# Two-layer graph attention on one core: gathering the neighbours of row blocks 0 to 2 in two portions, split by source column

## Chip, cores and metric

One core of a Trainium2 chip runs the whole kernel. The metric is device time in microseconds (us). PE is TensorE, DVE VectorE, ACT ScalarE, POOL GpSimd and SP SyncE, which here only starts transfers.

## The reference, cut to what matters

```python
N, D, H = 2048, 512, 16
x = layernorm(x + gnn0(x, adj, pairs, Wq, bq, Wk, bk))   # first layer: neighbour mean, corrected for few listed pairs
seq = (x @ W_seq).reshape(N, H, 32)
s1, s2 = einsum('nhd,d->hn', seq, a1), einsum('nhd,d->hn', seq, a2)
scores = leaky_relu(s1[:, :, None] + s2[:, None, :], 0.2) + (1 - adj) * -65500
hidden = einsum('hij,jhd->ihd', softmax(scores), seq).reshape(N, 512) @ W_out + b_out
out = layernorm(x + elu(hidden))
```

`adj` is 2048 x 2048 with ones on the diagonal and else about 4 ones in a row of 2048. In the second layer row i needs the rows of `seq` (and the score s2) of its neighbours j only.

## The kernel before, in words

The 2048 rows are 16 row blocks of 128 (one row per partition). Engines work from written-out queues and meet at semaphores. The stages, in order of time:

- **Listing and first product (0 to about 153 us).** SP loads the rows of `adj`. ACT casts a block to f16 (`cast_row`, L1006), PE transposes it (`turn_rows`, L621), ACT copies the transposed block out of PSUM (`save_turned`, L1015), and PE multiplies it with x (`multiply`, L639). Beside it DVE lists each row's neighbours (`listing`: `list_keys`, `list_rest`, `list_top`): the f16 key of column j is j+1, MAX8 finds the largest 8 of each eighth of the row, and `list_top` finds the largest 8, strikes them out (MATCH_REPLACE8) and finds the next 8. They go to `ek`. The f16 row buffer has two halves, so ACT casts block b only when block b-2 is listed (`row_listed`) and turned. POOL fetches adjacency values for the 10,000 pairs, 79 gathers of one value per partition (L530), and every group of 6 of them waits for a count of finished products (`ax_made`). `count_pairs` on DVE waits for the last of them, and most of what follows until the flag that says whether the sparse path can be used (`flag_made`) hangs on it.
- **Norm stage (about 157 to 231 us).** For each of the 16 blocks PE transposes the normed rows, computes `seq` with the scores s1 and s2 in 16 matmuls (`make_seq`, L841) and spreads the list of the block before over the partitions (`spread_keys`, L851). ACT saves the result, and SP stores each block of `seq` with s2, 528 f32 per row, to the table `seqtab` in device memory (L475). DVE norms rows, makes the span masks for the spreading (`make_key_span`) and, for four blocks at a time, the gather indices `eidx` (`pick_edges`). A block's 128 rows have at most KE x 128 = 512 neighbours beyond the first of each row. They are packed into four tiles of 128, one neighbour per partition; the first (nearest) neighbour of each row has a tile of its own, whose partition is the row itself (`near`). So a block takes GE = 5 gathers of 128 rows.
- **Second layer (from about 231 us).** POOL waits until all 16 blocks are in `seqtab` and then issues 5 indirect gathers for each block in turn (L607), into one of GR = 3 buffers. Block b from 3 on waits also until PE has summed block b-3 (`e_agg`). For a block DVE computes the arguments of the exponential (`arguments`, L1970, L1973, L1978), ACT takes the exponential (L1229, L1231), DVE multiplies the gathered rows by the weights (`weigh`, L2006, in lots), lays the row's own share and adds the nearest tile in PSUM (`own_share` L1929, `add_nearest` L1936), PE sums the packed tiles through one-hot matrices (L955, made by `one_hots` L1845), and DVE divides (`finish`, L1940 and L1942). `W_out`, ELU and the last norm follow some blocks behind (`add_elu`, L1876, L1878). Block 0 is done in two parts, its first three tiles ahead of the last two. At the start, `self_args` and `largest` (L1947 to L1964) make the largest scores.

## Time and profile before

| | us |
|---|---|
| time, median of 3 (lowest to highest) | 394.93 (393.57 to 396.96) |
| time of the profiled execution | 395.34 |
| its span | 393.5 |
| PE, DVE, ACT, POOL busy | 344.1, 322.2, 199.8, 186.6 |
| mean granted TensorE clock (1 is full speed) | 0.968 |

The profile is of one execution, the one of 395.34 us. Its span goes from the first to the last recorded instruction; 1.84 us lie around it. Times within it are counted from its start. A row of the timeline gives start, duration, engine, line, operation, what is written and read, how many instructions are merged, and in square brackets how long the engine had been idle before and what released it.

### The profile page before, as it was taken

The numbers are of one execution on the slowest core, as the hardware profiler recorded it, in microseconds if no ns is written. First come the engines' busy times: TensorE is split into PE (matmuls) and PEld (weight loads), VectorE is DVE, ScalarE is ACT, GpSimd is POOL, SyncE is SP. The second block draws the span as 40 slices with busy tenths as digits, with TensorE's granted clock in tenths as the row PEclk, the third lists the DMA queues.
The fourth block names the chain that finished last, engine by engine and source line by source line (L and its number), as shares of the span: only waits on it lengthen the run. The fifth ranks groups of instructions, "written<-read, shape, count | busy, mean of one in ns | idle before, by whom it ended". The sixth has DMA issues, their size and how long they took to land.

```text
span 393.5 us, 5227 instructions
## 1 busy us (share of the span) xinstructions
PE 344.1 (87%) x1656; PEld 213.8 (54%) x1656; DVE 322.2 (82%) x816; ACT 199.8 (51%) x449; POOL 186.6 (47%) x178
## 2 busy tenths in 40 slices
PE   0899899999999988999999934699989999999970
PEld 0444645555444644788888813456545655665540
DVE  2999999985978477777988687778899999999772
ACT  3975874466430224555654321122446776677780
POOL 7776558777771000000000047888778878770000
PEclk9999999999999999999999975899999999999995
DMA  6999464436994402921111237665675776662014
GB/s 250 373 384 378 177 214 121 185 126 160 229 231 92 145 0 66 383 106 66 57 55 57 82 110 209 177 171 161 172 191 164 201 215 209 182 205 82 27 56 142
DMA packets 34758, 65.10 MB, mean 165 GB/s; under 512 B 15649, under 2 KB 16801, under 8 KB 32673
## 3 DMA queue, kind: packets, MB, share of 16 engines
q1 hardware_dynamic: 25632, 42.45, 32.1%
q0 software_dynamic: 9088, 22.20, 20.5%
q8 instruction: 17, 0.28, 0.3%
q14 instruction: 21, 0.16, 0.1%
HBM read 53.50 MB, written 8.52 MB: 158 GB/s over the span
## 4 chain that ended last, share of the span: by engine, by line
PE 41%; DVE 26%; POOL 13%; issue 7%; ACT 6%; DMA 5%; SPq 0%; DVEq 0%; ACTq 0%; POOLq 0%
PE ps L639 17%; PE ps L841 15%; POOL adjT L607 9%; DVE adjT L2006 8%; POOL pr L530 5%; DMA arenaA<-in_x_dram 2%; DVE arenaC L1878 2%; DVE adjT L1876 2%; DVE ps L1936 2%; DVE arenaA L1942 2%; DVE ps L1929 2%; PE ps L621 2%; PE ps L830 2%; DVE arenaB L1845 2%; ACT adjT L1015 1%
## 5 line engine op out<-in xcount | busy, mean ns | idle before, releaser
L639 PE MATMUL ps<-arenaB,adjT 128*128 128x512 f16 x512 | 115.6, 379 | 2.7 <-ACT adjT L1015 1.6
L530 POOL DMA_INDIRECT pr<-in_adj_dram,aidx x79 | 82.0, 1038 | 30.6 <-issue 23.0
L607 POOL DMA_INDIRECT adjT<-seqtab,eidx x64 | 77.2, 1206 | 19.5 <-issue 19.5
L955 PE MATMUL ps<-adjT,arenaB 128*128 128x264 f32 x256 | 67.9, 412 | 18.5 <-DVE adjT L2006 14.1
L639 PEld LDWEIGHTS ps<-arenaB,adjT 128*128 128x128 f16 x512 | 48.8, 98 | 59.9 <-ACT adjT L1015 3.2
L607 POOL DMA_INDIRECT adjT<-seqtab,near x16 | 21.5, 1341 | 107.6 <-DMA seqtab<-arenaA 102.9
L955 PEld LDWEIGHTS ps<-adjT,arenaB 128*128 128x128 f32 x256 | 49.4, 200 | 41.1 <-DVE ps L1936 21.1
L841 PE MATMUL ps<-stage 128*128 128x272 f32 x256 | 61.5, 394 | 0.1
L868 PE MATMUL ps<-adjT 128*128 128x512 f32 x120 | 54.1, 593 | 1.0 <-ACT ps L1135 1.0
L841 PEld LDWEIGHTS ps<-stage 128*128 128x128 f32 x256 | 47.4, 190 | 9.5 <-ACT stage L1104 0.8
L2006 DVE TENSOR_TENSOR adjT<-adjT 128x1024 f32<-128x1024 f32 (+2 forms) x35 | 47.9, 1373 | 2.3 <-ACT adjT L1231 1.9
L1006 ACT ACTIVATE halves<-stage 128x2048 f16<-128x2048 f32 x16 | 30.8, 1922 | 13.2 <-DMA stage<-in_adj_dram 6.1
L868 PEld LDWEIGHTS ps<-adjT 128*128 128x128 f32 x120 | 21.6, 190 | 22.8 <-issue 21.5
L1015 ACT COPY adjT<-ps 128x1024 f16<-128x1024 f16 x20 | 19.2, 1014 | 21.5 <-PE ps L621 21.5
L1323 DVE TENSOR_TENSOR arenaA<-iota,halves 128x2048 f16<-128x2048 f16 x15 | 18.3, 1223 | 7.5 <-ACT halves L1006 7.4
L1135 ACT COPY ps<-adjT 128x512 f32<-128x512 f32 x15 | 8.8, 590 | 30.4 <-DVE adjT L1876 30.4
L621 PE MATMUL ps<-identh,halves 128*128 128x128 f16 x176 | 13.2, 235 | 9.7 <-ACT halves L1006 9.7
L1330 DVE MAX8 arenaA<-arenaA 128x8 f16<-128x256 f16 x60 | 21.1, 414 | 0.5
L1229 ACT ACTIVATE stage<-stage 128x80 f32<-128x80 f32 (+2 forms) x17 | 4.4, 258 | 32.9 <-DVE stage L1978 32.9
L1335 DVE MAX8 arenaA<-arenaA 128x8 f16<-128x256 f16 x60 | 20.8, 411 | 0.0
L1110 ACT COPY arenaA<-ps 128x256 f32<-128x256 f32 x32 | 11.9, 375 | 14.8 <-PE ps L841 14.8
L621 PEld LDWEIGHTS ps<-identh,halves 128*128 128x128 f16 x176 | 12.1, 106 | 12.1 <-issue 9.1
(277 smaller groups left out, 486.7 us busy)
## 6 DMA issues: line engine op xcount, KB each, us to landing
stage<-in_adj_dram SPq DMA_DIRECT2D x16, 1024.0 KB, 6.1
seqtab<-arenaA SPq DMA_DIRECT2D x16, 264.0 KB, 2.0
arenaA<-in_x_dram SPq DMA_DIRECT2D x4, 1024.0 KB, 12.0
out_dram<-arenaC SPq DMA_DIRECT2D x16, 256.0 KB, 3.5
arenaB<-in_x_dram SPq DMA_DIRECT2D x1, 1536.0 KB, 10.6
pr<-in_adj_dram,aidx POOLq DMA_INDIRECT x79
arenaC<-in_L_gnn_Wq_dram SPq DMA_DIRECT2D x1, 1024.0 KB, 16.6
arenaC<-in_L_gnn_Wk_dram SPq DMA_DIRECT2D x1, 1024.0 KB, 20.0
```

The lines of the kernel that those rows point to most:

```text
L530: g.indirect_dma_start(out=avals[:, t:t + 1], out_offset=None, in_=adj_flat, in_offset=bass.IndirectOffsetOnAxis(ap=aidx[:, t:t + 1], axis ...
L607: g.indirect_dma_start(out=Grow[:, b % GR, k, :], out_offset=None, in_=seqtab, in_offset=bass.IndirectOffsetOnAxis(ap=source, axis=0)).the ...
L621: ins = t.transpose(turn_banks(b)[:, j, :], arowh[:, b % 2, j * P:(j + 1) * P], identh[:])
L639: ins = t.matmul(bank(4 + b % 2), adjT[:, b, j, :], xsplit[:, w, j, :], start=(j == 0 and w == 0), stop=(j == NB - 1 and w == 1))
L841: ins = t.matmul(half_bank(n), xT[:, b % 2, k, :], Wx[:, k, s, :], start=(k == 0), stop=(k == KT - 1))
L868: ins = t.matmul(bank(6 + b % 2), hT[:, b % 2, k, :], Wo[:, k, :], start=False, stop=(k == KT - 1), skip_group_check=True)
L955: ins = t.matmul(bank(2 * (b % 2) + c, HALF), ehot[:, b % HOTS, k - 1, :], Grow[:, b % GR, k, c * HALF:(c + 1) * HALF], start=False, stop= ...
L1006: s.activation(arowh[:, b % 2, :], arow[:, b % 2, :], ACT.Identity, accum_out=deg[:, 0, b:b + 1]).then_inc(row_cast, 1)
L1015: s.copy(adjT[:, b, 8 * k:8 * k + 8, :], turn_banks(b)[:, 8 * k:8 * k + 8, :]).then_inc(row_evac, 1)
L1330: v.max(top[:, 0, 8 * k:8 * k + 8], key[:, k * SEG:(k + 1) * SEG])
L1335: ins = v.max(top[:, 0, 8 * k:8 * k + 8], key[:, k * SEG:(k + 1) * SEG])
L2006: v.tensor_tensor(some[:, :, 0:D1], some[:, :, 0:D1], some[:, :, D1:HW].to_broadcast([P, (last - first) * H1, D1]), ALU.mult).then_inc(e_m ...
```

## The change

The neighbours of row blocks 0, 1 and 2 (`EARLY` = 3) are split by column. Those in the first `CUT` = 13 blocks of columns ("low") fill the nearest tile and the first three packed tiles, those in the last three blocks ("high") the fourth packed tile.

- POOL waits for the first 13 stores of the table (a semaphore of their own, `tab_first`) and issues the 4 low gathers of each of the three blocks. Then it waits for the last three stores and issues one high gather for each. Blocks 3 to 15 are gathered as before.
- For blocks 0 to 2, `list_top` has two more instructions, which turn the key j+1 into 2048-j, so that the lowest columns rank first. A new function `split_lists` (13 instructions) counts the low neighbours of each row, and turns the keys back.
- The counts that PE sums (`count_rows`) have three more columns, `measure` and `judge` one and two more instructions, `make_key_span` one for blocks 0 to 2, `pick_edges` one for the first group. The spread list has a column more (51 for 50).
- In the second layer blocks 0 to 2 are done in two parts, the four low tiles and the high one. The start is in another order: the arguments of block 0 come ahead of what the row's own share needs, and DVE waits for the whole table only after them. The one-hots of blocks 3 to 5 move from ahead of block 0 into blocks 0 to 2, and one call of `largest` from block 2 to block 3.

```diff
             def list_top(b, top=top, junk=junk):
...
-                link(v.max(ek[:, b, 0:8], top[:, 0]))
-                link(v.match_replace(top[:, 1], ek[:, b, 0:8], top[:, 0], 0.0))
-                v.max(ek[:, b, 8:16], top[:, 1])
+                found, rest = top[:, 0], top[:, 1]
+                if b < EARLY:
+                    link(v.tensor_scalar(top[:, 1], top[:, 0], -1.0, N + 1.0, ALU.mult, ALU.add))
+                    link(v.scalar_tensor_tensor(top[:, 1], top[:, 0], 0.0, top[:, 1], ALU.is_gt, ALU.mult))
+                    found, rest = top[:, 1], top[:, 0]
+                link(v.max(ek[:, b, 0:8], found))
+                link(v.match_replace(rest, ek[:, b, 0:8], found, 0.0))
+                v.max(ek[:, b, 8:16], rest)
...
             listing(NB - 2)
+            split_lists()
             list_keys(NB - 1)
...
                 def make_key_span(b):
...
+                    n = KE * P
+                    if b < EARLY:
+                        n -= P
+                        v.tensor_scalar(span[:, b % 2, n:], iota[:, n:n + P], hend[:, 0, b:b + 1], hend[:, 1, b:b + 1],
+                                        ALU.max, ALU.min)
...
-                pool.wait_ge(tab_store, 16 * NB)
-                for b in range(NB):
+                pool.wait_ge(edges_made, 1)
+                pool.wait_ge(tab_first, 16 * CUT)
+                for b in range(EARLY):
+                    for k in range(KE):
+                        gather(b, k, e_low[b])
+                pool.wait_ge(tab_store, 16 * (NB - CUT))
+                for b in range(EARLY):
+                    gather(b, KE, e_high[b])
+                for b in range(EARLY, NB):
                     if b % 4 == 0:
                         pool.wait_ge(edges_made, b // 4 + 1)
-                    if b >= GR:
-                        pool.wait_ge(e_agg, b - GR + 1)
+                    pool.wait_ge(e_agg, b - GR + 1)
                     for k in range(GE):
...
-                    for b in range(3, 6):
-                        one_hots(b)
-                    own_share(0)
-                    for lo, hi in parts_of(0):
-                        dve.wait_ge(e_first[lo // FEW], 16 * (hi - lo))
-                        arguments(0, lo, hi)
-                        weigh(0, lo, hi)
-                    for b in range(1, NB):
-                        if b == 1:
+                    for b in range(EARLY):
+                        dve.wait_ge(e_low[b], 16 * KE)
+                        arguments(b, 0, KE)
+                        if b == 0:
+                            self_rest()
+                            table_stored(dve)
+                            late(v.memset(seq[:, :, :, D1:HW], 1.0))
+                            self_parts()
+                            own_share(0)
+                        one_hots(EARLY + b)
+                        if b == 2:
+                            own_share(2)
+                        weigh(b, 0, KE)
+                        dve.wait_ge(e_high[b], 16)
+                        arguments(b, KE, GE)
+                        if b == 0:
                             own_share(1)
-                        dve.wait_ge(e_gather[b % GR], 16 * GE * (b // GR + (b % GR > 0)))
+                        else:
+                            finish(b - 1)
+                        weigh(b, KE, GE)
+                    for b in range(EARLY, NB):
+                        dve.wait_ge(e_gather[b % GR], 16 * GE * (b // GR))
                         arguments(b, 0, GE)
```

The queues show this at three places. On DVE, the end of a block's listing in the first stage, here block 1; `arenaA` holds the 64 candidate keys, `ekb` the list. Before:

```order
L1340 TENSOR_REDUCE over<-arenaA 128x1
L1341 MAX ekb<-arenaA 128x8
L1342 MATCH_REPLACE arenaA<-ekb,arenaA 128x64
L1343 MAX ekb<-arenaA 128x8
L1344 ISA arenaA,deg<-halves,identh 128x128
L1344 ISA deg 128x1
```

After, at the same place:

```order
L1365 TENSOR_REDUCE over<-arenaA 128x1
L1368 TENSOR_SCALAR arenaA<-arenaA 128x64
L1369 SCALAR_TENSOR_TENSOR arenaA<-arenaA 128x64
L1371 MAX ekb<-arenaA 128x8
L1372 MATCH_REPLACE arenaA<-ekb,arenaA 128x64
L1373 MAX ekb<-arenaA 128x8
L1374 ISA arenaA,deg<-halves,identh 128x128
L1374 ISA deg 128x1
```

Two instructions of 64 elements stand between the reduction and the first MAX, for blocks 0, 1 and 2 each.

On POOL, the first gathers of the second layer; `near` is the nearest tile, `eidx` a packed one. Before:

```order
L607 DMA adjT<-seqtab,near 128x528 [waits edges_made,tab_store]
L607 DMA adjT<-seqtab,eidx 128x528 x4
L607 DMA adjT<-seqtab,near 128x528
L607 DMA adjT<-seqtab,eidx 128x528 x4
L607 DMA adjT<-seqtab,near 128x528
L607 DMA adjT<-seqtab,eidx 128x528 x4
L607 DMA adjT<-seqtab,near 128x528 [waits e_agg]
```

After:

```order
L615 DMA adjT<-seqtab,near 128x528 [waits tab_first,edges_made]
L615 DMA adjT<-seqtab,eidx 128x528 x3
L615 DMA adjT<-seqtab,near 128x528
L615 DMA adjT<-seqtab,eidx 128x528 x3
L615 DMA adjT<-seqtab,near 128x528
L615 DMA adjT<-seqtab,eidx 128x528 x3
L615 DMA adjT<-seqtab,eidx 128x528 [waits tab_store]
L615 DMA adjT<-seqtab,eidx 128x528 x2
L615 DMA adjT<-seqtab,near 128x528 [waits e_agg]
```

Twelve of the fifteen gathers now wait for 13 stores, and three for all 16; the first gather of block 3 still waits for block 0's sums.

On DVE, the start of the second layer, from the first wait for gathered rows to the first weighing of block 1. Before (block 0 in parts of 3 and 2 tiles):

```order
L1970 TENSOR_TENSOR stage<-arenaB,adjT 128x48 [waits e_first0]
L1973 SCALAR_TENSOR_TENSOR stage<-stage 128x48 [waits sp_arg]
L1978 TENSOR_TENSOR stage<-stage,arenaB 128x48 [waits mxe_made,sp_arg]
L2006 TENSOR_TENSOR adjT<-adjT 128x16x32 [waits e_exp]
L1936 TENSOR_TENSOR ps<-ps,adjT 128x2x264 [waits e_mul,own_laid]
L2006 TENSOR_TENSOR adjT<-adjT 128x16x32 x2
L1970 TENSOR_TENSOR stage<-arenaB,adjT 128x32 [waits e_first1]
```

After (the part of 4 tiles, with what now stands inside it):

```order
L2043 TENSOR_TENSOR stage<-arenaB,adjT 128x64 [waits e_low0]
L2046 SCALAR_TENSOR_TENSOR stage<-stage 128x64 [waits sp_arg]
L2051 TENSOR_TENSOR stage<-stage,arenaB 128x64 [waits mxe_made,sp_arg]
L2020 TENSOR_TENSOR arenaB<-arenaB 128x256
L2022 TENSOR_SCALAR arenaB<-arenaB 128x256 [waits self_arg]
L2086 MEMSET arenaA 128x256 [waits tab_store,tab_first]
L2027 TENSOR_TENSOR arenaB<-arenaB,deg 128x256 [waits self_exp,late_link]
L1993 TENSOR_TENSOR ps<-arenaA,arenaB 128x2x264 [waits opened,self_kept]
L1909 TENSOR_TENSOR arenaB<-iota,erow 128x512
L2074 TENSOR_TENSOR adjT<-adjT 128x16x32 [waits e_exp]
L2000 TENSOR_TENSOR ps<-ps,adjT 128x2x264 [waits e_mul,own_laid]
L2074 TENSOR_TENSOR adjT<-adjT 128x16x32 x3
```

The own-share preparation moves behind the arguments of block 0, and one one-hot build (L1909) stands there for three.

## Rows read from the trace of the kernel before

**Rows 1.** Stretches: core us, busy us (instructions) by engine, clock, DMA share, GB/s.

```profile
231.40:278.10 46.70, 32.34 (x115) 22.33 (x116) 36.37 (x66) 8.19 (x21) 36.98 (x32) 0.82 0.63 178
...
290.00:360.00 70.00, 66.95 (x242) 41.66 (x241) 67.83 (x108) 47.21 (x128) 51.32 (x40) 1.00 0.64 186
```

**Rows 2.** Timeline of DVE: first of the second layer, arguments of blocks 3, 4, 5.

```profile
231.44 0.42 DVE L1947 TENSOR_TENSOR arenaB<-scores,M 128x256 f32<-128x256 f32 x1 [0.76 <-DVE M L1906]
...
262.11 0.30 DVE L1970 TENSOR_TENSOR stage<-arenaB,adjT 128x80 f32<-128x80 f32 x1 [2.14 <-DMA adjT<-seqtab,eidx]
...
269.23 0.30 DVE L1970 TENSOR_TENSOR stage<-arenaB,adjT 128x80 f32<-128x80 f32 x1 [0.95 <-DMA adjT<-seqtab,eidx]
...
278.09 0.30 DVE L1970 TENSOR_TENSOR stage<-arenaB,adjT 128x80 f32<-128x80 f32 x1 [1.36 <-DMA adjT<-seqtab,eidx]
```

**Rows 3.** Timeline of POOL: first gather of blocks 0, 3, 4, 5, 6.

```profile
230.45 0.97 POOL L607 DMA_INDIRECT adjT<-seqtab,near  x1 [102.87 <-DMA seqtab<-arenaA]
...
250.22 2.18 POOL L607 DMA_INDIRECT adjT<-seqtab,near  x1 [0.30 <-issue]
...
259.41 0.95 POOL L607 DMA_INDIRECT adjT<-seqtab,near  x1 [0.30 <-issue]
...
266.03 2.17 POOL L607 DMA_INDIRECT adjT<-seqtab,near  x1 [0.31 <-issue]
...
275.63 0.95 POOL L607 DMA_INDIRECT adjT<-seqtab,near  x1 [0.30 <-issue]
```

**Rows 4.** DMA issues (count, KB each, us to landing); SP's timeline, last four stores.

```profile
seqtab<-arenaA SPq DMA_DIRECT2D x16, 264.0 KB, 2.0
adjT<-seqtab,eidx POOLq DMA_INDIRECT x64, 3.9
...
215.65 12.84 SPq L475 DMA_DIRECT2D seqtab<-arenaA  x4
```

**Rows 5.** Timeline, a gather beside a weighing; POOL's group of the first stage (busy us, mean ns).

```profile
247.87 1.23 DVE L2006 TENSOR_TENSOR adjT<-adjT 128x1024 f32<-128x1024 f32 x1 [0.71 <-ACT adjT L1231]
248.33 1.59 POOL L607 DMA_INDIRECT adjT<-seqtab,eidx  x1 [0.30 <-issue]
...
L530 POOL DMA_INDIRECT pr<-in_adj_dram,aidx x79 | 82.0, 1038 | 30.6 <-issue 23.0
```

**Rows 6.** Last stretch of the norm stage, columns as in Rows 1.

```profile
216.00:228.00 12.00, 11.72 (x64) 9.40 (x62) 8.31 (x30) 4.22 (x18) 0.00 (x0) 1.00 0.18 68
```

**Rows 7.** DVE groups by shape, 231.4 to 278.1 us: count, busy us, mean ns.

```profile
L1929 DVE TENSOR_TENSOR ps<-arenaA,arenaB 128x528 f32<-128x528 f32 x5 | 3.6, 717 | 0.0
...
L2006 DVE TENSOR_TENSOR adjT<-adjT 128x512 f32<-128x512 f32 x5 | 3.3, 697 | 1.2 <-ACT adjT L1231 1.2
```

**Rows 8.** Timeline of PE: block 0's 16 matmuls of packed tiles.

```profile
241.08 5.91 PE L955 MATMUL ps<-adjT,arenaB 128*128 128x264 f32 x16 [10.05 <-DVE adjT L2006]
```

**Rows 9.** Timelines of DVE, ACT, PE and POOL, 31 to 52 us, engine by engine.

```profile
35.56 0.22 DVE L1341 MAX8 ekb<-arenaA 128x8 f16<-128x64 f16 x1
35.81 0.09 DVE L1342 MATCH_VALUE_LOAD arenaA<-ekb,arenaA 128x8 f16 x1
...
36.48 0.08 DVE L1344 DVE_READ_ACCUMULATOR2_ANT deg<- 128x1 f32 x1
...
31.41 1.91 ACT L1006 ACTIVATE halves<-stage 128x2048 f16<-128x2048 f32 x1 [0.72 <-DVE deg L1344]
...
36.67 1.91 ACT L1006 ACTIVATE halves<-stage 128x2048 f16<-128x2048 f32 x1 [3.26 <-PE ps L621]
...
40.55 1.04 PE L639 MATMUL ps<-arenaB,adjT 128*128 128x512 f16 x4 [1.37 <-ACT adjT L1015]
...
51.91 0.95 POOL L530 DMA_INDIRECT pr<-in_adj_dram,aidx  x1 [5.53 <-PE ps L639]
```

**Rows 10.** Timeline of DVE around the listing of the last block.

```profile
116.43 1.23 DVE L1323 TENSOR_TENSOR arenaA<-iota,halves 128x2048 f16<-128x2048 f16 x1 [2.14 <-ACT halves L1006]
...
119.89 0.24 DVE L1365 TENSOR_TENSOR arenaA<-prf 128x79 f32<-128x79 f32 x1 [0.54 <-DMA pr<-in_adj_dram,aidx]
```

More of the change, by code:

```diff
@@ L47, in two_layer_graph_attention @@
     GR = 3
-    KW = 18 + 32
-    FEW = 3
+    KW = 18 + 32 + 1
+    EARLY = 3
+    CUT = NB - 3
     HOTS = 8
@@ L300, in parts_of, with nth_part, table_stored @@
         def parts_of(b):
-            return ((0, FEW), (FEW, GE)) if b == 0 else ((0, GE),)
+            return ((0, KE), (KE, GE)) if b < EARLY else ((0, GE),)
+        def nth_part(b, lo):
+            return sum(len(parts_of(a)) for a in range(b)) + 1 + (lo > 0)
+        def table_stored(eng):
+            eng.wait_ge(tab_first, 16 * CUT)
+            eng.wait_ge(tab_store, 16 * (NB - CUT))
         def lots_of(b):
-            return tuple((k, k + 1) for k in range(GE)) if b == 0 else ((0, 2), (2, GE))
+            if b == 0:
+                return tuple((k, k + 1) for k in range(GE))
+            return ((0, 2), (2, KE), (KE, GE)) if b < EARLY else ((0, 2), (2, GE))
         def weighed(b, k):
@@ L714, in count_rows @@
                 pe.wait_ge(cnt_made, 1)
-                t.matmul(ps[:, 3, 0:NB], below[:], mv[:, :, 0], start=True, stop=True)
-                t.matmul(ps[:, 3, NB:2 * NB], ones[:], mv[:, :, 0], start=True, stop=True)
+                n = NB + EARLY
+                t.matmul(ps[:, 3, 0:n], below[:], counts[:, 0, :], start=True, stop=True)
+                t.matmul(ps[:, 3, n:2 * n], ones[:], counts[:, 1, :], start=True, stop=True)
                 pe.wait_ge(u_saved, 1)
@@ L1231, in act_second_layer @@
                             s.activation(G[:, b % GR, lo * H1:hi * H1, D1], a2, ACT.Exp, scale=-1.0).then_inc(e_exp, 1)
+                            if n == 1:
+                                act.wait_ge(self_made, 1)
+                                s.activation(sa[:, 2], sa[:, 1], ACT.Exp).then_inc(self_exp, 1)
                         if b >= 2:
@@ L1830, in pick_edges @@
                         link(ins)
+                        if c == 0:
+                            last = spot[:, 0].rearrange("p (q k) -> p q k", q=4)[:, 0:EARLY, KE - 1]
+                            starts = sp_.rearrange("p (q k) c -> p q k c", q=4)[:, 0:EARLY, KE - 1, KW - 1]
+                            link(v.scalar_tensor_tensor(last, rowid[:, KE - 1:KE].to_broadcast([P, EARLY]), 2.0, starts,
+                                                        ALU.add, ALU.subtract))
                         link(v.tensor_tensor(pick[:, 0], kiota.unsqueeze(1).to_broadcast([P, 4 * KE, 16]),
```

96 lines of the change are left out of this document (60 added, 36 removed).

## The prediction

> **What bounds the kernel now.** I read the stretches first, then the waits of DVE and POOL, then the chain of waits back from the end. The second layer is the part that the change speaks of. In its first 46.7 us, to 278.1, DVE is busy for 36.4 us and POOL is issuing nearly all the time; from 290 to 360 us DVE is busy for 67.8 of 70 us [rows 1]. So this layer has two bounds, one behind the other. At first it is the issue of gathers: DVE reaches the arguments of blocks 3, 4 and 5 and waits 2.14, 0.95 and 1.36 us for the last gather [rows 2], while POOL, which waited for the last store until 230.45, sits only 0.30 us between two gathers [rows 3]. From block 6 on no argument waits for a gather, and DVE's own work sets the pace. Whatever makes block 5's arguments start earlier than 278.09 is therefore passed on to the end, and what comes earlier only on POOL is not.
>
> Ahead of the second layer the norm stage is PE's: 11.72 of 12 us busy, while DVE has 8.31 and POOL nothing [rows 6]. In the first stage one chain matters for the edits there, and I come to it below.
>
> **The gathers, part by part.** SP issues the last four stores from 215.65, so block 12's is the one at 215.65; a store lands in 2.0 us [rows 4]. The low gathers can start at 215.65 + 2.0 + 0.3 = 217.95 instead of 230.45, 12.5 us earlier. A gather and the gap behind it take 0.95 + 0.30 = 1.25 us when nothing disturbs it [rows 3], so the 12 low ones would end at 233.0. One that starts while DVE multiplies two operands out of SBUF is held: at 248.33 a gather began inside a weighing that ended at 249.10, and took 1.59 us, to 0.82 after that end [rows 5]. The norm stage has such instructions too, but short ones. I take 0.1 us a gather, as in the first stage, where 79 gathers took 1.04 us in the mean beside DVE's listing [rows 5], hence 234.2; by bounds 0 and, if each met one of 0.72 us [rows 7], 0.7 us a gather, 241.4. The three high gathers follow, and 3.9 us after its issue [rows 4] the first has landed, at 238.1. DVE asks for it at about 241.5 (below): not late.
>
> DVE's side now. From 231.44 block 0 costs: five instructions of 0.42 (L1947 and its like) 2.1; arguments 0.8; the four that prepare the own share, up to 0.42 each, and ACT's exponential between them 2.0; own share 0.7, one one-hot build, taken as an own share, 0.7; the nearest tile 0.7 and its addition 0.7; the first packed tile 0.7. That is 239.8, and PE can begin its sums. Then two more tiles at 0.7, the arguments of the high tile 0.6 (at 241.8), the next own share 0.7 and the high tile 0.7: block 0 leaves DVE at 243.2 [rows 2, 7]. Block 1 is two sets of arguments 1.4, one-hots 0.7, weighing 1.2 + 1.2 + 0.7, the addition 0.7 and a division 0.9, together 6.8; block 2 the same with an own share, 7.5. So DVE alone would be at block 3's arguments at 257.5. Block 3 took 269.23 - 262.11 - 0.95 = 6.2 us without its wait, and gets the moved call of `largest`, 0.8; block 4 took 278.09 - 269.23 - 1.36 = 7.5 [rows 2]. DVE alone would begin block 5 at 257.5 + 7.0 + 7.5 = 272.0, 6.1 us earlier than before.
>
> But POOL is in it again, through the three buffers: block 3 is gathered only when PE has summed block 0. PE's 16 matmuls for it took 5.91 us [rows 8], in a stretch whose mean granted clock is 0.82 [rows 1]. From 239.8 they end at 245.7, and POOL begins block 3 at 246, 4.2 us earlier than 250.22 and not 12.5. Before, the first six blocks took (275.63 - 230.45)/6 = 7.5 us each on POOL, and blocks 3 to 5 8.5, since a denser DVE holds more gathers [rows 3]; I take 7.8. Block 5's first gather is at 246 + 15.6 = 261.6. From its first gather to its arguments a block needed 11.9, 9.8 and 12.1 us (blocks 3, 4, 5) [rows 2, 3], mean 11.3: 272.9. That is later than DVE's own 272.0, so POOL decides, by a little, and the gain is 278.09 - 272.9 = 5.2 us. The best that it can be is 6.1, DVE's own; with 8.5 us a block and 12.1 behind it 275.1, a gain of 3.0; with block 0's sums no earlier than before (247) and POOL's worst block, 266.03 to 275.63, three times over, 278.3, none.
>
> **What it costs ahead of that.** The two instructions in `list_top` are linked, each waiting for the one before. The step from one linked instruction on 64 elements to the next is 0.25 us, from 35.56 to 35.81 [rows 9]; two of them, 0.45 (the first overlaps the reduction), in three blocks 1.35 us by 36.5 us. This DVE time is on the path. ACT may cast block 4 only when block 2 is listed: DVE's last instruction of that listing ends at 36.56 and the cast starts at 36.67. The row gives PE as the releaser, because a transpose ends in the same moment, but the cast needed only transposes long done; the cast of block 3, at 31.41, names DVE [rows 9]. Behind the cast stand ACT's copy of block 3's transpose, and PE, which waits 1.37 us for it until 40.55; behind PE's block 3 the pair gathers, which stood for 5.53 us until 51.91. From there POOL issues them at its own pace to the last, and DVE waits for that one's landing until 119.89 [rows 9, 10]. None of these has slack, so I let 1.35 us through to the end; by bounds 0, if some of it finds a gap that I do not see, and 1.7, a quarter more.
>
> `split_lists` is 13 instructions. Its cover is in two waits: DVE stood for 2.14 us before the last listing and for 0.54 us before `count_pairs`, 2.68 in all [rows 10]. The instructions are on 3 to 48 elements, eight of them linked; at 0.2 and 0.1 they make 2.2 us, at 0.25 each 3.3. So 0 to 0.6 comes out; I take 0.1. The additions to `measure` and `judge` stand behind the flag's inputs and beside PE's last product: 0, by bounds up to 0.3. The extra span instruction for blocks 0 to 2 sits at the start of the norm stage, where DVE is only just ahead of PE: 0.15 us, by bounds 0 to 0.5. The extra instruction in `pick_edges` and the wider lists find DVE with a third of its time free and cost nothing; without that cover they would be 0.2.
>
> The sum is 395.34 - 5.2 + 1.35 + 0.1 + 0.15 = 391.7 us for the profiled execution. That execution was 0.4 above the median of the runs, so a median would be 391.3 by the same steps. I say 391.4, 0.9% below 394.93.
>
> **A rule weighed.** Beside gathers DVE's own instructions were no longer than without: own share, addition and one-hots run at 0.7 us with POOL issuing. The Trainium skill, page "SBUF — State Buffer", section "Who interferes with whom", states that VectorE and GpSimd share a port pair under an exclusive lock, that whoever issues first has it for the whole instruction, and that a `tensor_tensor` contends only with what GpSimd reads. The held gather agrees as far as POOL is the loser [rows 5]; for DVE as the loser no row shows a case, and by that half of the rule the moved gathers would lengthen the norm stage. It is the last rival.
>
> **Rivals.** First, the listing is hidden: the wait view is right that the cast of block 4 was PE's, or PE's later waits take the 1.35 us up. For it speaks the releaser in the row, against it the missing slack behind. Then 395.34 - 5.2 + 0.25 = 390.4, by the median 390.0.
>
> Second, the issue of gathers keeps the bound: the held gathers of blocks 3 to 5 stay as in the rows, 8.5 us a block, or block 0's sums come no earlier because PE is as slow and starts later. The gain is 3.0 or less, on average 1.7: 395.3. From 1.6 us of gain down the change is no gain at all. For it speaks that POOL is never idle before and that a denser DVE holds it more; against, that it then has the pause from 238 to 246.
>
> Third, and slower: the high gather of block 0 is late. It stands behind 12 low ones, and DVE has block 0's high tile, the next own share and all of block 1 queued behind that wait. If every low gather meets a DVE instruction of 0.7 us, the first high one is issued at 241.4, and with a landing drawn out to 5 us beside the last stores and held itself for 1.2 us it is there at 248, 6 us after 241.8. That takes the whole gain, and 1.6 us of cost stays: 397. It decides from about 3.6 us of lateness on, a landing at 245.4.
>
> Fourth, DVE is the loser of the lock: each of 12 gathers holds up one DVE instruction by up to 0.95 us, 11.4 us, of which the 12 us stretch hides 12 - 8.3 = 3.7 [rows 6]. The norm stage then ends 7.7 us later: 399. With half of that blocking, 2.0 us later, the time would be 393.7.
>
> **How the numbers follow.** Forecast 0.50, listing hidden 0.14, issue-bound 0.24, late high tile 0.06, DVE held 0.06. The forecast's own range is 390.0 to 393.0. A measurement of this kernel tells about 1% from no change, 3.9 us, and 1% faster is 391.0, close under the forecast: I give the forecast 0.24 of its 0.50 there, the hidden listing all of its 0.14, and the issue-bound case none, which makes 0.38 for faster by over 1%. Slower by over 1% (above 398.9) needs most of the fourth rival or more than the third's price: 0.04. The rest, 0.58, is within 1%. The range of 8 in 10 goes from 389.4, a little under the hidden listing, to 395.6, which takes in the issue-bound case.
>
> **What would show it.** POOL's first gather of the table some 12 to 13 us before the last block's store lands, and 12 gathers of about 1.3 us with their gaps. Then a pause of POOL of 6 to 9 us, ended by PE's sums of block 0. DVE's arguments of blocks 1 and 2 without a wait for a gather, and those of block 5 some 40.5 to 42.5 us behind the layer's first instruction, where it was 46.65. The cast of block 4 at 38.0 for 36.67, and `count_pairs` at 121.2 for 119.9. The start of the second layer at about 233.0 for 231.44. The forecast is wrong if that start is not later (listing hidden), if it is over 3 us later (DVE held), or if block 5's arguments still come 45 us or more behind it.

## The result, and the profile after

| | before | changed |
|---|---|---|
| time, median (lowest to highest), us | 395.28 (393.57 to 396.96), 4 runs | 2285.93 (2284.49 to 2286.89), 4 runs |
| time and span of the profiled execution | 395.34, 393.5 | 2284.49, 2282.7 |
| mean granted TensorE clock | 0.968 | 0.570 |

The ratio is 5.781 (95% interval 5.762 to 5.800). Times here and below are medians of all runs, while a ratio takes only those runs of each kernel that lie within 1.5% of its fastest, so it can differ from the ratio of the medians. The prediction was 391.4 us, 389.4 to 395.6, with 0.04 on slower. No case of it comes near.

This is the changed kernel's page: its span, the first section's busy times, the clock of section 2 in 40 slices, four groups of section 5, and one row of the DMA issues.

```profile
span 2282.7 us, 23174 instructions
PE 2054.1 (90%) x9616; PEld 1921.5 (84%) x9616; DVE 1780.3 (78%) x1558; ACT 162.0 (7%) x305; POOL 88.2 (4%) x98
...
PEclk9999555555555555555555555555555555555587
...
L920 PE MATMUL ps<-arenaB 128*128 128x33 f32 x8192 | 1751.0, 402 | 146.4 <-DVE arenaB L2164 146.4
...
L2164 DVE TENSOR_TENSOR arenaB<-arenaB,adjT 128x2048 f32<-128x2048 f32 x256 | 586.7, 2292 | 131.2 <-PE ps L920 122.1
L2159 DVE SCALAR_TENSOR_TENSOR arenaB<-stage,arenaB 128x2048 f32<-128x2048 f32 x256 | 601.8, 2351 | 9.1
L2157 DVE TENSOR_SCALAR arenaB<-stage,arenaB 128x2048 f32<-128x2048 f32 x256 | 329.4, 1287 | 17.0 <-DMA stage<-etab 6.5
...
stage<-etab SPq DMA_DIRECT2D x32, 1024.0 KB, 5.5
```

Read it for what is there and for what is not. PE has 8192 records from one line that the kernel before never reached, in 256 batches of 32 (16 heads by 16 source blocks); `etab` is a table that only the dense second layer writes. No row of any view has `seqtab` as the source of a gather, so nothing of what [rows 3] show happens at all, early or late. The kernel took the other branch of its second layer: the flag that says "the lists do not fit, work with the whole matrix" was up. That dense branch stands in the kernel before too, and had not run there.

Up to the branch the trace is the predicted one, a little late. Below are the changed kernel's casts of blocks 3 and 4 and the restart of the pair gathers, which answer to [rows 9], the first use of the gathered pairs [rows 10], the copy that closes the norm stage, and the first instruction of the dense layer.

```profile
32.79 1.91 ACT L1030 ACTIVATE halves<-stage 128x2048 f16<-128x2048 f32 x1 [0.46 <-DVE deg L1374]
...
38.56 1.91 ACT L1030 ACTIVATE halves<-stage 128x2048 f16<-128x2048 f32 x1 [3.76 <-DVE deg L1374]
...
53.80 0.94 POOL L545 DMA_INDIRECT pr<-in_adj_dram,aidx  x1 [5.64 <-PE ps L662]
...
122.40 0.24 DVE L1414 TENSOR_TENSOR arenaA<-prf 128x79 f32<-128x79 f32 x1 [0.40 <-DMA pr<-in_adj_dram,aidx]
...
233.12 0.17 DVE L1970 COPY M<-ps 128x16 f32<-128x16 f32 x1
237.07 0.43 DVE L2134 TENSOR_TENSOR arenaB<-scores,M 128x256 f32<-128x256 f32 x1 [3.78 <-issue]
```

The same copy in the kernel before:

```profile
230.51 0.17 DVE L1906 COPY M<-ps 128x16 f32<-128x16 f32 x1
```

So 2.6 of the 1890 us are front cost, and all the rest lies behind the copy, from which the changed kernel needs 2049.6 us to its end, and the kernel before 163.0. From 400 us to the end, says the stretch below, PE is busy for 1707 of 1882 us at a mean clock of 0.52.

```profile
400.00:2282.00 1882.00, 1707.17 (x7811) 1661.62 (x7811) 1470.67 (x878) 38.82 (x68) 0.00 (x0) 0.52 0.05 19
```

**Why the flag is up.** `judge` raises it when a row block has more than KE * P = 512 listed neighbours beyond the nearest. The count comes from `count_rows`, which multiplies `counts` with a matrix of ones, and so adds it up over the 128 partitions. `split_lists` adds a constant to `counts` on every partition, to fold the two portions' own limits into the one test: 128.0 for the low portion, 384.0 for the high. Summed over 128 partitions these are 16384 and 49152. Both are above 512 whatever the graph is. What was meant is 128 and 384 on the sum of a block. An excess of 128 over the block is 1.0 a partition, one of 384 is 3.0, KE - 1. With these the test reads low + 128 > 512 and high + 384 > 512, which is what three tiles and one tile hold. The input fits: blocks 0 to 2 have 295, 259 and 312 low extra neighbours (room for 384) and 81, 104 and 88 high ones (room for 128), and the largest block has 428.

### The profile page after: what moved, and what is told of

It reads as the page before. It is cut to its first block, busy times and chain, and to the rows that moved or that the text cites. A ratio compares the mean times of both kernels' runs of the same rounds, so it can differ in the third digit from the quotient of the medians.

```text
span 2282.7 us, 23174 instructions
## 1 busy us (share of the span) xinstructions
PE 2054.1 (90%) x9616; PEld 1921.5 (84%) x9616; DVE 1780.3 (78%) x1558; ACT 162.0 (7%) x305; POOL 88.2 (4%) x98
## 4 chain that ended last, share of the span: by engine, by line
PE 85%; DVE 7%; issue 2%; ACT 2%; POOL 1%; DMA 1%; DVEq 0%; SPq 0%; ACTq 0%; POOLq 0%
PE ps L920 77%; PE ps L892 3%; PE ps L865 2%; DVE arenaB L2159 2%; DVE arenaB L2164 2%; POOL pr L545 1%; PE ps L662 1%; DVE arenaB L2157 1%; DMA arenaA<-in_x_dram 0%; ACT adjT L1168 0%; ACT ps L1159 0%; ACT adjT L1150 0%; DVE arenaA L2173 0%; DVE arenaB L1343 0%; PE ps L912 0%
## 5 line engine op out<-in xcount | busy, mean ns | idle before, releaser
L920 PE MATMUL ps<-arenaB 128*128 128x33 f32 x8192 | 1751.0, 402 | 146.4 <-DVE arenaB L2164 146.4
L920 PEld LDWEIGHTS ps<-arenaB 128*128 128x128 f32 x8192 | 1748.8, 333 | 148.9 <-DVE arenaB L2164 148.9
L2164 DVE TENSOR_TENSOR arenaB<-arenaB,adjT 128x2048 f32<-128x2048 f32 x256 | 586.7, 2292 | 131.2 <-PE ps L920 122.1
L2159 DVE SCALAR_TENSOR_TENSOR arenaB<-stage,arenaB 128x2048 f32<-128x2048 f32 x256 | 601.8, 2351 | 9.1
L2157 DVE TENSOR_SCALAR arenaB<-stage,arenaB 128x2048 f32<-128x2048 f32 x256 | 329.4, 1287 | 17.0 <-DMA stage<-etab 6.5
L892 PE MATMUL ps<-adjT 128*128 128x512 f32 x128 | 70.9, 706 | 35.9 <-ACT adjT L1150 35.9
L892 PEld LDWEIGHTS ps<-adjT 128*128 128x128 f32 x128 | 27.3, 223 | 70.2 <-issue 37.1
L1940 DVE SCALAR_TENSOR_TENSOR adjT<-ps,adjT 128x512 f32<-128x512 f32 x16 | 11.1, 691 | 81.2 <-ACT adjT L1170 81.2
L1854 DVE BATCH_NORM_STATS2 stats<-arenaC 128x6 f32<-128x512 f32 x32 | 22.2, 694 | 1.1
L1355 DVE MAX8 arenaA<-arenaA 128x8 f16<-128x256 f16 x60 | 21.1, 414 | 0.5
## 6 DMA issues: line engine op xcount, KB each, us to landing
arenaB<-in_x_dram SPq DMA_DIRECT2D x1, 1536.0 KB, 10.7
```

The costliest lines, as they stand in the source:

```text
L892: ins = t.matmul(bank(6 + b % 2), hT[:, b % 2, k, :], Wo[:, k, :], start=False, stop=(k == KT - 1), skip_group_check=True)
L920: ins = t.matmul(ps[:, b // 8, (b % 8) * (D1 + 1):(b % 8 + 1) * (D1 + 1)], p_buf[:, j % 2, b * P:(b + 1) * P], seqh[:, j, :], start=(j == ...
L1355: v.max(top[:, 0, 8 * k:8 * k + 8], key[:, k * SEG:(k + 1) * SEG])
L1854: link(v.bn_stats(stats[:, b, :], x1[:, b, :]))
L2157: v.tensor_scalar(p_raw, eB[:, 0, :], Fh[:, 0, j:j + 1], None, ALU.mult).then_inc(L.sem, 1)
L2159: v.scalar_tensor_tensor(p_raw, eB[:, 1, :], Fh[:, 1, j:j + 1], p_raw, ALU.mult, ALU.max).then_inc(L.sem, 1)
```

## The experiments

**e1, both constants mended.**

```diff
-                v.tensor_scalar_add(counts[:, 1, 0:EARLY], counts[:, 0, 0:EARLY], float(P))
+                v.tensor_scalar_add(counts[:, 1, 0:EARLY], counts[:, 0, 0:EARLY], 1.0)
...
-                v.tensor_scalar_add(counts[:, 1, NB:NB + EARLY], counts[:, 0, NB:NB + EARLY], float((KE - 1) * P))
+                v.tensor_scalar_add(counts[:, 1, NB:NB + EARLY], counts[:, 0, NB:NB + EARLY], float(KE - 1))
...
+                        gather(b, k, e_low[b], CUT * P)
```

(The last line names only the first 13 blocks of the table as the source of the low gathers; the rows they fetch are the same. It is part of e1 and of e5 to e12. It can't have to do with the flag, since no gather of the table runs while the flag is up.)

> The changed kernel with the added numbers 128 and 384 in split_lists replaced by 1 and 3 (both are added on each of 128 partitions and then summed over the partitions), and the low gathers given the first 13 blocks of the table as their source. Theory A (the sum over partitions makes 128 x 128 out of the 128, so the count is always over the limit of 512, and the kernel takes its dense path): the sparse path is back, about 391 to 393 us, with POOL's first table gather near 220 us. Theory B (the split lists do not fit their tiles for these data, or the sparse path of the change is itself slow): 2286 us again, or far over 400 us. Rival within A: the gain of the early gathers is eaten by the front (count_pairs was 2.5 us later in the changed kernel): 395 us.

Measured: 391.24 us (390.01 to 392.93), ratio 0.9895 (0.9866 to 0.9925). 1895 us are gone with two numbers, and the change as it was meant is 1.05% faster than the kernel before. The timeline of POOL and then of DVE, as in [rows 3] and [rows 2]:

```profile
222.03 0.95 POOL L615 DMA_INDIRECT adjT<-seqtab,near  x1 [91.78 <-DMA seqtab<-arenaA]
...
249.39 1.15 POOL L615 DMA_INDIRECT adjT<-seqtab,near  x1 [8.36 <-PE ps L979]
...
233.36 0.17 DVE L1970 COPY M<-ps 128x16 f32<-128x16 f32 x1
234.38 0.42 DVE L2011 TENSOR_TENSOR arenaB<-scores,M 128x256 f32<-128x256 f32 x1 [0.85 <-DVE M L1970]
...
258.91 0.30 DVE L2043 TENSOR_TENSOR stage<-arenaB,adjT 128x80 f32<-128x80 f32 x1 [0.17 <-DMA adjT<-seqtab,eidx]
...
266.06 0.31 DVE L2043 TENSOR_TENSOR stage<-arenaB,adjT 128x80 f32<-128x80 f32 x1 [0.20 <-DMA adjT<-seqtab,eidx]
...
275.08 0.30 DVE L2043 TENSOR_TENSOR stage<-arenaB,adjT 128x80 f32<-128x80 f32 x1 [1.52 <-DMA adjT<-seqtab,eidx]
```

The first gather is 12.35 us ahead of the layer's first instruction, POOL then stands for 8.36 us until PE has summed block 0, and block 5's arguments come 40.70 us behind the layer's start, where it was 46.65.

**e2, the low constant alone mended; e3, the kernel before with the limit set to 0** (nothing else of the change; its flag is up too).

```diff
-                link(v.tensor_scalar(bad[:, 2:3], bad[:, 2:3], float(KE * P), None, ALU.is_gt))
+                link(v.tensor_scalar(bad[:, 2:3], bad[:, 2:3], 0.0, None, ALU.is_gt))
```

> The changed kernel with only the first number mended (1 for 128), the 384 of the high counts left. Theory A: 384 x 128 = 49152 is over 512 by itself, so the dense path is still taken: 2286 us. Theory A', that only the low count raised the flag: about 392 us.

> The kernel before with the limit of the packed count at 0 for 512, so that its flag is always raised; nothing else is changed. Theory A: the whole of 2286 us is the dense path of the second layer, so this takes the changed kernel's time less what the change costs ahead of the second layer: 2283 to 2285 us. Theory B (something of the change is slow): clearly under 2280 us.

Measured: 2282.74 and 2284.10 us, one run each. The costliest group of e2's page, then that of e3's, whose line numbers are those of the kernel before:

```profile
L920 PE MATMUL ps<-arenaB 128*128 128x33 f32 x8192 | 1751.0, 402 | 146.5 <-DVE arenaB L2164 146.5
```

```profile
L896 PE MATMUL ps<-arenaB 128*128 128x33 f32 x8192 | 1751.0, 402 | 146.0 <-DVE arenaB L2086 146.0
```

So the 384 alone is enough to raise the flag. That the 128 alone would be follows from the same sum, 16384 over 512, and was not run. The whole excess is the dense branch's ordinary price, which the kernel before pays as well when it is sent there. The cause is settled. What follows asks whether the steps of the prediction hold for the change as it was meant.

**e4, the kernel before with the two linked instructions in the first three lists, and nothing else.**

```diff
+                if b < 3:
+                    link(v.tensor_scalar(top[:, 1], top[:, 0], -1.0, N + 1.0, ALU.mult, ALU.add))
+                    link(v.scalar_tensor_tensor(top[:, 1], top[:, 0], 0.0, top[:, 1], ALU.is_gt, ALU.mult))
```

> The kernel before with only the two linked 64-element instructions of list_top added for blocks 0 to 2, writing what nobody reads. If the listing is on the path as I predicted: 1.35 us more, 396.6 beside 395.3. If it is hidden: no change. If more is behind it (the changed kernel's count_pairs came 2.5 us later): 2.5 us more, 397.8.

Measured: 397.06 us against 395.35, ratio 1.0046 (1.0026 to 1.0066), +1.7 us. Cast, restart of the pair gathers, first use of the pairs, as in [rows 9, 10]:

```profile
38.05 1.91 ACT L1006 ACTIVATE halves<-stage 128x2048 f16<-128x2048 f32 x1 [3.76 <-DVE deg L1347]
...
53.29 0.94 POOL L530 DMA_INDIRECT pr<-in_adj_dram,aidx  x1 [5.63 <-PE ps L639]
...
121.33 0.24 DVE L1368 TENSOR_TENSOR arenaA<-prf 128x79 f32<-128x79 f32 x1 [0.50 <-DMA pr<-in_adj_dram,aidx]
```

All three are 1.38 to 1.44 us later than before, and so is the copy that closes the norm stage (231.90, 1.39 later). Nothing on the way takes any of it up. And the cast now names DVE as its releaser, where the row of before named a transpose that ended in the same moment.

This trace shows one thing more. Behind the copy e4 is the kernel before, instruction for instruction. Yet from the copy to the end of the span it needs 161.90 us and the kernel before 162.99, because other gathers met a weighing: those of blocks 3 to 5 took 5.1 us over 0.95 each in e4, and 6.6 us in the kernel before. Differences of about 1 us between two such stretches say nothing by themselves.

**e5 to e8, measured in one set.** That set ran under other conditions: the kernel before took 414.72 us in it (407.09 to 417.09, 17 runs), 5% more than in the other sets, and the first use of the gathered pairs, at 119.9 to 122.6 us in them, comes at 137.0 to 141.3 in the four profiles here. So their totals say little, and I read them from the copy that closes the norm stage to the end of the span. That stretch is 162.99 us in the kernel before (161.90 in e4) and 157.24 in e1. For the kernel before it is known only from the other set. The stretch carries over from one set to the other: e6 needs 155.91 us for it in this one, and its repetition e10, below, 156.10.

e5 lets the first gather wait for the whole table:

```diff
-                pool.wait_ge(tab_first, 16 * CUT)
+                table_stored(pool)
```

> The kernel of e1 with one line changed: the first gather of blocks 0 to 2 waits for all 16 stores of the table, not for the first 13. Everything else of the split (two portions of arguments and weights, the key and count edits) stays. Theory A, the gain is the early start alone: the first table gather moves from 222.03 to about 233.5 us, the 15 gathers of blocks 0 to 2 end 12 us later, block 5's arguments come 46 to 47 us behind the layer's first instruction as before, and the kernel costs before plus the front's cost: 396.5 to 398 us. Rival B, the gain comes from the new order of the DVE's work (own shares, self term, one-hots moved): it stays at 391 to 393 us.

Measured: 420.24 us, ratio 1.0221 (1.0100 to 1.0342); the stretch 166.69 us, 9.4 more than e1, with block 5's arguments 50.20 us behind the layer's start. DVE's waits for block 0's low and high portions:

```profile
259.89 0.27 DVE L2043 TENSOR_TENSOR stage<-arenaB,adjT 128x64 f32<-128x64 f32 x1 [5.32 <-DMA adjT<-seqtab,eidx]
...
271.11 0.19 DVE L2043 TENSOR_TENSOR stage<-arenaB,adjT 128x16 f32<-128x16 f32 x1 [4.23 <-DMA adjT<-seqtab,eidx]
```

e1 has neither. Rival B falls. The expectation of theory A was low too: without the early start the new order is not the old one back but 3.7 us worse (4.8 against e4's stretch), because block 0's high tile now stands behind twelve low ones. That is the third rival of the prediction, seen where the early start doesn't cover it.

e6 lists blocks 0 to 2 against numbers that run downwards, so that the two linked instructions go:

```diff
+            g.iota(iotar, [[-1, N]], base=N, channel_multiplier=0,
+                   allow_small_or_imprecise_dtypes=True).then_inc(rev_made, 1)
...
-                link(v.tensor_tensor(key, iota[:], arowh[:, b % 2, :], ALU.mult))
+                link(v.tensor_tensor(key, iotar if b < EARLY else iota[:], arowh[:, b % 2, :], ALU.mult))
```

> The kernel of e1, but the rows of blocks 0 to 2 are listed against a second table of numbers that runs downwards (made once by POOL in the first microseconds), so the two 64-element instructions in each of the three lists go. Theory A, these six instructions lie on the chain that starts POOL's 79 pair gathers: the casts come back to 31.4 and 36.7 us, the pair gathers start at about 51.9 instead of 53.2, and the time is 1.2 to 1.8 us below e1's 391.2, so 389.4 to 390.0. Rival B, the front has slack somewhere behind (for instance the landing of the last pair gather, which waited 2.04 us in e1): within 0.4 us of e1, 390.8 to 391.6.

Measured: 420.53 us, ratio 1.0267 (1.0180 to 1.0354). That says nothing on the listing, since e1 did not run in that set, and the kernel is repeated as e10. But its trace showed something new at the end of the norm stage (ACT, then DVE, which waits for it):

```profile
258.71 0.37 ACT L1138 COPY arenaA<-ps 128x256 f32<-128x256 f32 x1 [8.12 <-remote]
...
259.20 0.58 DVE L1963 TENSOR_REDUCE gm<-arenaA 128x16 f32<-128x256 f32 x1 [8.19 <-ACT arenaA L1140]
```

ACT stood for 8.12 us while the early gathers were out ("remote" is a releaser that this profile does not hold). e7 has the same stop with 7.37 us and e8 with 7.51; e5, without early gathers, has none, nor has e1. In this set none of the three kernels with the early start is faster than the kernel before (ratios 1.008 to 1.027), so the gain of e1 is shown for the other conditions only.

e7 takes blocks 1 and 2 in one portion. Beside changes of the order of DVE's work, the line that decides is:

```diff
-            return ((0, KE), (KE, GE)) if b < EARLY else ((0, GE),)
+            return ((0, KE), (KE, GE)) if b == 0 else ((0, GE),)
```

> The kernel of e1, but only block 0 is taken in two portions; blocks 1 and 2 wait for their high tile too and are worked in one piece, which saves DVE three 16-column instructions and one weighing instruction a block, about 0.55 us each, 1.1 together. In e1 the high tiles were there before block 1 began, so the wait costs nothing. Theory A, behind block 0 it is POOL, released by PE's sums of block 0, that sets the time: DVE reaches block 3's arguments 1.1 us earlier and waits 1.1 us more for its gathers, and the time stays within 0.4 us of e1: 390.8 to 391.6. Rival B, DVE sets the time: 390.0 to 390.4.

Measured: 417.89 us, ratio 1.0143 (0.9998 to 1.0289); the stretch 158.49 us. Block 3's arguments:

```profile
284.95 0.30 DVE L2043 TENSOR_TENSOR stage<-arenaB,adjT 128x80 f32<-128x80 f32 x1 [3.13 <-DMA adjT<-seqtab,eidx]
```

It spares DVE work and waits 3.13 us at the next gather, where e1 waited 0.17. DVE is ready for block 3 at 24.41 us behind the copy, 0.97 earlier than in e1, and gets it 1.99 us later, since block 3's five gathers were held for 2.40 us in all, for 0.37 in e1. Rival B falls: there is no gain. The stretch is 1.25 us longer, more than the 0.4 that theory A allowed, but not clear of the 1 us seen between equal stretches.

e8 keeps PE at work ahead of block 0's sums:

```diff
+                        if b == 0:
+                            pe.wait_ge(self_arg, 3)
+                            keep_warm(16)
                         pe.wait_ge(e_own, b + 1)
+                        if b == 0:
+                            keep_warm(8)
```

> The kernel of e1, with 24 matmuls of nobody's use (128x512, f16) on PE between the norm stage and block 0's sums, in a bank that is opened anew afterwards. In e1 PE stood idle there for 8.5 us and then worked off block 0's 16 matmuls at a granted clock of 0.50, 780 ns each where others take 386, ending at 249.1; POOL's block 3 waits for that. Theory A, this wait is the bound: with the clock at 1.00 block 0's sums end about 247, POOL's block 3 starts 2 us earlier, DVE's waits for gathers of blocks 3 to 5 (1.9 us in e1) all but go, and the time is 1.2 to 1.9 us below e1: 389.3 to 390.0. Rival B, DVE is the bound already and only waits elsewhere: 390.8 to 391.6.

Measured: 416.97 us, ratio 1.0077 (1.0004 to 1.0150); the stretch 157.79 us. The profile is of a run of 418.61 us, one of the longer of twelve. First block 0's sums in e1, with the stretch in which most of them ran (PE's busy time and count, granted clock, DMA share, GB/s), then the sums in e8, a gather of block 3 that was held, and DVE's arguments of block 5:

```profile
242.36 6.75 PE L979 MATMUL ps<-adjT,arenaB 128*128 128x264 f32 x16 [8.48 <-DVE adjT L2074]
...
244.00:248.00 4.00, 4.00 (x11) 0.50 0.00 0
```

```profile
269.18 3.72 PE L989 MATMUL ps<-adjT,arenaB 128*128 128x264 f32 x16
...
274.65 1.65 POOL L615 DMA_INDIRECT adjT<-seqtab,eidx  x1 [0.30 <-issue]
...
301.17 0.30 DVE L2053 TENSOR_TENSOR stage<-arenaB,adjT 128x80 f32<-128x80 f32 x1 [2.41 <-DMA adjT<-seqtab,eidx]
```

In e1 PE had stood for 8.48 us and worked most of them off at half of the full clock (1.2 of 2.4 GHz). In e8 the 16 matmuls take 3.72 us and not 6.75, and POOL's block 3 starts 14.06 us behind the copy and not 16.03: the first half of theory A is right. The gain is then lost. Of the lead of 1.97 us, 1.43 go in gathers of blocks 3 to 5 that are held for longer (5.69 us over 0.95 each in all, for 4.26), and the last gather of block 5 lands 3.80 us behind its end for 2.92. So block 5's arguments wait 2.41 us (1.52 in e1), and the stretch is no shorter. POOL issues without a pause from block 0's sums to block 5, but an earlier start is not passed on through that queue.

e9, the same kernel as e1 (below), says the same more closely. Its block 3 starts at 14.94 behind the copy, 0.88 later than e8's, and block 4 at 21.44 for 21.42: the whole difference is gone within five gathers.

**e9 to e12, measured in one set,** under the conditions of e1 again (before 395.05 us, 11 runs). e9 is e1's kernel and e10 is e6's. e11 issues only block 0's four low gathers early:

```diff
-                for b in range(EARLY):
-                    for k in range(KE):
-                        gather(b, k, e_low[b], CUT * P)
+                for k in range(KE):
+                    gather(0, k, e_low[0], CUT * P)
                 pool.wait_ge(tab_store, 16 * (NB - CUT))
-                for b in range(EARLY):
-                    gather(b, KE, e_high[b])
+                gather(0, KE, e_high[0])
+                for b in range(1, EARLY):
+                    for k in range(KE):
+                        gather(b, k, e_low[b])
+                    gather(b, KE, e_high[b])
```

and e12 is e10 with that edit.

> The kernel of e1, unchanged, beside the next three on one chip. The chip of e5 to e8 ran the kernel before in 414.7 us and not in 395.4, and three of its four profiles (those with early gathers) show ACT stopped for 7.4 to 8.1 us in the last block of the norm stage, while the twelve early gathers were out, with nothing in the profile that ends the stop; e1 showed none. Theory A, the stop is the early burst's work, on chips that are slow to serve it: on such a chip (before near 415) it is there again and e9 is 1 to 2% slower than before, on one like e1's (before near 395) it is absent and the ratio is 0.987 to 0.993 again. Rival B, the stop belongs to the edits of e6 to e8: e9 has none on any chip.

> The kernel of e6, now beside e9. Theory A, the six short listing instructions of blocks 0 to 2 lie on the chain that starts POOL's 79 pair gathers: 1.2 to 1.8 us below e9 on the same chip, 389.4 to 390.0 where before takes 395.4, with the casts at 31.4 and 36.7 us. Rival B, slack behind them: within 0.4 us of e9.

> The kernel of e1, but only block 0's four low gathers are issued inside the norm stage; the other eight and the three high ones wait for the whole table and go block by block. The burst shrinks from 15 us to 5, block 0's arguments still find their rows, and the 11 later gathers, issued from about the layer's start at 1.25 us each, should land before blocks 1 and 2 want them (11.7 and 18.3 us behind the copy of the maxima) and be out before block 0's sums end (16.0). Theory A, the early start pays through block 0 alone: the stretch from the copy of the maxima to the end stays within 1 us of e1's 157.2, and ACT's stop, where e9 shows one, is under 3 us. Rival B, the gain needs all twelve ahead: the stretch is 2 us or more longer and block 1 or 2 waits for gathers.

> e10 and e11 together. By theory A of both it has neither the listing's 1.4 us nor the long burst: 1.2 to 1.8 us below e11, and where before takes 395.4 it comes to 389.3 to 390.5; on a chip with the stop it is the first version that is not slower than before. By the rivals it is no faster than the better of e10 and e11.

| | time, us | ratio (95% interval) | copy to end, us |
|---|---|---|---|
| e9, mended | 391.03 | 0.9918 (0.9891 to 0.9944) | 156.78 |
| e10, reversed numbers | 389.58 | 0.9858 (0.9834 to 0.9882) | 156.10 |
| e11, four early | 391.51 | 0.9920 (0.9898 to 0.9942) | 157.40 |
| e12, both | 390.14 | 0.9878 (0.9852 to 0.9903) | 157.13 |

e9 repeats e1, and none of the four has ACT's stop. e10's cast of block 4 and its restart of POOL are back where [rows 9] have them:

```profile
36.66 1.91 ACT L1034 ACTIVATE halves<-stage 128x2048 f16<-128x2048 f32 x1 [3.26 <-PE ps L648]
...
51.90 0.95 POOL L549 DMA_INDIRECT pr<-in_adj_dram,aidx  x1 [4.38 <-PE ps L666]
```

and it is 1.45 us faster than e9: theory A, and the fastest kernel of this study, 1.4% under the kernel before. The difference is one of medians. In the profiled execution (390.86 us, the longest of five) the gain is lost again at the pairs, where the last gather took 1.95 us and first use is at 122.15. e12 against e11 shows the gain in the traces too: first use at 120.33 for 121.27, and the copy at 231.07 for 232.10. e11 shows how little of the early start is needed. POOL stops after four gathers and goes on with block 0's high one when the table is whole:

```profile
224.56 0.95 POOL L615 DMA_INDIRECT adjT<-seqtab,eidx  x1 [0.30 <-issue]
232.04 0.97 POOL L615 DMA_INDIRECT adjT<-seqtab,eidx  x1 [6.53 <-DMA seqtab<-arenaA]
```

No argument of blocks 0 to 4 waits for a gather, and the stretch is 0.6 us longer than e9's. e12 gains 1.37 over e11, but nothing over e10.

## Why the prediction was wrong, point by point

**The step that failed** is the one on the counts and the flag: "The additions to `measure` and `judge` stand behind the flag's inputs and beside PE's last product: 0, by bounds up to 0.3." It priced the edited counts as instructions, as it did `split_lists`, where the two constants stand, and never worked out their value. What it put at 0 sends the second layer down the dense branch: 2049.6 us from the copy to the end for 163.0. The step took the branch of [rows 2] and [rows 3] for granted; e1 to e3 show that the constants alone decide between 391 and 2285 us. A branch was in plain sight in the diff, with the limit of 512 beside a constant of 384 that goes through a sum over 128 partitions. The rivals had no case in which the change doesn't do what it says, and so nothing bounded the upper end. What that case costs could not be read from the trace of before, which has no row of the dense branch. e3 gives it: 2284.10 us.

**The early gathers, for the mended kernel.** The gain was put at 5.2 us. It is 5.75 in e1 and 6.21 in e9, from the copy to the end, against the one profile of the kernel before; against e4's stretch it is 4.66 and 5.12. By the medians e10, which has the early start without the listing's cost, is 5.47 under the kernel before. The size was right within what can be told. The first gather, put at 217.95, came 1.3 us later than the front's delay explains (221.05 in e9, whose norm stage ends 1.8 us later than before). The sum took the 2.0 us in which a store lands in the median of 16; the thirteenth took 2.8 in e9, and the rest of the 1.3 is between its landing and the gather. This cost nothing, as POOL has a pause behind. "POOL begins block 3 at 246", that is 14.6 us behind the layer's first instruction: 13.9 in e9 and 15.0 in e1. PE began block 0's sums 8.0 us behind it, for 8.4 in the sum, and took 5.63 and 6.75 us for the 5.91 taken over from before. Block 0 left DVE at 10.7 us from the layer's start for the 11.8 predicted. Block 5's arguments came 40.70 us (e1) and 39.99 (e9) behind it, for 40.5 to 42.5. The pace of blocks 3 to 5 on POOL, put at 7.8 us, was (272.47 - 249.39)/3 = 7.7 in e1 and 7.9 in e9.

**"Passed on to the end"** is the step that holds best. The prediction said that whatever makes block 5's arguments start earlier is passed on to the end. From these arguments to the end of the span there are 115.1 to 115.8 us in each of the eleven traces of the sparse branch, whether the arguments came 40.8 or 51.2 us behind the copy.

**"POOL decides, by a little"** was right: three waits of 1.9 us in all are left in e1, one of 1.3 in e9. But the chain does not pass on what I thought. I had the time of block 0's sums go through to block 5; in e8 they ended 2 us earlier than in e1, and nothing was won. What is between is held gathers. Most of the holding in e1 is in block 5's own, beside DVE's weighing:

```profile
262.87 2.13 POOL L615 DMA_INDIRECT adjT<-seqtab,near  x1 [0.30 <-issue]
...
267.81 1.88 POOL L615 DMA_INDIRECT adjT<-seqtab,eidx  x1 [0.30 <-issue]
...
269.59 1.75 DVE L2074 TENSOR_TENSOR adjT<-adjT 128x1536 f32<-128x1536 f32 x1
269.99 2.17 POOL L615 DMA_INDIRECT adjT<-seqtab,eidx  x1 [0.30 <-issue]
```

Three of its five gathers take 0.9 to 1.2 us more than 0.95. It is not this hold that eats e8's lead: in e8 it is 3.08 us in all, in e1 3.33. The lead goes in blocks 3 and 4, held for 1.09 and 1.52 us in e8 and 0.37 and 0.56 in e1, and in the longer landing. That a gather is held while a weighing runs is read from such rows; no run removed it, and what would be won without it is not shown.

**The front.** The listing, put at 1.35 us, measured 1.38 to 1.44 in the trace of e4, 1.7 in its time, and 1.45 in e10 against e9, between medians. The rival "listing hidden" is out. `split_lists` stood in its cover, as said: DVE still waits for the landing of the pairs, 2.04 us in e1 and 0.18 in e9. From the first use of the pairs to the copy the mended kernel needs 110.75 us for 110.62 before: the key spans and the count edits together cost 0.13, for 0.15 predicted. What is over in e1 (first use at 122.61, 121.57 in e9) is a landing 4.05 us behind the end of the last pair gather, for 2.48 in e9 and 2.65 before; nothing here explains it.

**DVE as the loser of the lock.** The Trainium skill, page "SBUF — State Buffer", section "Who interferes with whom", lets whoever issues first hold the shared ports. I gave that half of the rule 0.06. In e9 DVE is busy for 8.30 of the 12 us from 218 in the norm stage with 7.12 us of gathers beside it, and was for 8.31 without them [rows 6]. The rival's 7.7 us are not there.

## What to carry to other kernels

Where a diff touches a number that a branch depends on, work out that number for this input before any duration: what is summed over what, and on which side of the limit it falls. A branch that the trace of before never took is a rival with a price of its own, here over a hundred times that of any other. And work that comes earlier pays only until the next thing that holds the same queue: e7 moved DVE's and e8 POOL's by 1 to 2 us, and both lost it again in gathers that were held.

## What the runs showed that I had not expected

On the dense branch PE is busy for 90% of the span and yet shows a granted clock of one half of full speed (1.2 of 2.4 GHz) from the fifth slice on, some 230 us in, to the last two. Between batches of 32 matmuls it stands for DVE, 146.4 us in all over 256 batches.

An early gather can lengthen a DVE instruction, by little. In e1 this one began 0.45 us into the first gather and ended 0.11 us behind it:

```profile
222.03 0.95 POOL L615 DMA_INDIRECT adjT<-seqtab,near  x1 [91.78 <-DMA seqtab<-arenaA]
222.48 0.61 DVE L1877 TENSOR_SCALAR stage<-iota,eend 128x512 f16<-128x512 f16 x1 [0.42 <-PE ps L875]
```

It takes 0.41 us elsewhere. In e9 it met the same gather at 221.44 and took 0.41, so it isn't hit each time.

What stopped ACT for 7.4 to 8.1 us in e6, e7 and e8 stays open. Early gathers were out in all three, and the one kernel of that set without them had no such stop. But e6's own kernel, run again as e10 under the usual conditions, had none either, and in that set the first stage was slow as well. The record gives both sets the same chip number, so a slow chip, as e9's expectation has it, is not shown. e11 would have told it apart there, and ran in the other set.
